# The first attention's tasks in a new order, with transposes placed between the matmuls of the projections

## The reference

```python
x = x + _L0_xattn_ref(_layernorm(x, axis=-1), ctx_1024, ctx_1024, ...)

def _L0_xattn_ref(query, key, value, w_q, b_q, w_k, b_k, w_v, b_v, w_o, b_o):
    q = query @ w_q.T + b_q
    k = key @ w_k.T + b_k
    v = value @ w_v.T + b_v
    # 16 heads of 16 features
    scores = jnp.einsum('bhqd,bhkd->bhqk', q, k) * scale
    probs = jax.nn.softmax(scores, axis=-1)
    y = jnp.einsum('bhqk,bhkd->bhqd', probs, v)
    return y @ w_o.T + b_o
```

## Time and profile before

| | |
|---|---|
| median of the timed runs | 3880.64 us |
| span of the profiled execution, first to last instruction | 3869.9 us |
| the profiled execution's own time, outside its span | not given apart; the median is 10.7 us above the span |
| TensorE busy over the span | 3678.2 us, 95% |
| VectorE, ScalarE, GpSimd busy | 3088.5, 2207.4, 2200.5 us |
| mean granted TensorE clock | 0.981 |
| 500 to 700 us (first attention): TensorE, VectorE, ScalarE, GpSimd | 196.3, 176.9, 145.6, 138.1 of 200 us |

### The profile page before, as it was taken

How to read it: one execution, slowest core, us unless ns; L and a number is a source line. 1 busy time by engine, 2 the same in 40 slices (tenths; PEclk the granted TensorE clock), 3 DMA queues, 4 the chain that set the end, 5 groups by cost and what they waited for, 6 DMA issues and landing times. The chain is left out here.

```text
span 3869.9 us, 134428 instructions
## 1 busy us (share of the span) xinstructions
PE 3678.2 (95%) x47408; PEld 2870.0 (74%) x47408; DVE 3088.5 (80%) x5266; ACT 2207.4 (57%) x4529; POOL 2200.5 (57%) x3316
## 2 busy tenths in 40 slices
PE   5999999995799999999999996999999999999999
PEld 4777777773688888888888884566666668888888
DVE  4888888885778777778777775798888977777777
ACT  3777777775444444444444442577677765555554
POOL 5666666664245443333333334466666667887777
PEclk9999999997899999999999998899999999999999
DMA  4677777774332322222222224799999952232322
GB/s 130 197 204 207 214 209 209 205 213 154 102 85 79 84 68 74 66 70 69 68 72 68 72 66 90 158 211 216 211 217 208 215 151 80 75 77 75 79 75 72
DMA packets 834241, 502.59 MB, mean 130 GB/s; under 512 B 262037, under 2 KB 824408, under 8 KB 833480
## 3 DMA queue, kind: packets, MB, share of 16 engines
q1 hardware_dynamic: 832680, 493.49, 50.5%
q0 software_dynamic: 928, 0.49, 0.1%
HBM read 251.27 MB, written 214.96 MB: 120 GB/s over the span
## 5 line engine op out<-in xcount | busy, mean ns | idle before, releaser
L1556 ACT ACTIVATE phase_spare<-phase_loop_hid,phase_b1T 128x128 f32<-128x128 f32 x2048 | 586.1, 368 | 710.9 <-PE phase_loop_hid L193 702.2
L1129 DVE TENSOR_REDUCE phase_loop_mx<-phase_loop_score 128x8 f32<-128x1024 f32 x512 | 625.4, 1222 | 98.5 <-PE phase_loop_score L882 91.0
L1522 PE MATMUL phase_loop_moe_y<-phase_w,phase_spare 128*128 x2048 | 693.6, 379 | 0.1
L1037 ACT ACTIVATE phase_loop_pt<-phase_loop_scoreT 128x1024 f32<-128x1024 f32 x448 | 458.6, 1024 | 268.3 <-PE phase_loop_scoreT L916 265.8
L1524 PE MATMUL phase_loop_moe_y<-phase_w,phase_spare 128*128 x2048 | 558.2, 273 | 0.0
L191 PE MATMUL phase_loop_hid<-phase_loop_moe_h,all_w_first_hi 128*128 128x128 f16 x2048 | 449.2, 219 | 0.0
L192 PE MATMUL phase_loop_hid<-phase_loop_moe_h,all_w_first_hi 128*128 128x128 f16 x2048 | 449.1, 219 | 0.0
L192 PE MATMUL phase_loop_hid<-phase_loop_moe_h,phase_w_hi 128*128 128x128 f16 x2048 | 449.1, 219 | 0.0
L193 PE MATMUL phase_loop_hid<-phase_loop_moe_h,all_w_first_lo 128*128 128x128 f16 x2048 | 449.1, 219 | 0.0
L193 PE MATMUL phase_loop_hid<-phase_loop_moe_h,phase_w_lo 128*128 128x128 f16 x2048 | 449.1, 219 | 0.0
L191 PE MATMUL phase_loop_hid<-phase_loop_moe_h,phase_w_hi 128*128 128x128 f16 x2048 | 449.0, 219 | 0.0
(11 more groups left out here) (293 smaller groups left out, 11038.9 us busy)
## 6 DMA issues: line engine op xcount, KB each, us to landing
qk_scratch<-phase_loop_qk SPq DMA_DIRECT2D x192, 256.0 KB, 3.4
phase_loop_cin<-in_ctx SPq DMA_DIRECT2D x128, 256.0 KB, 4.6
x_scratch<-phase_loop_x SPq DMA_DIRECT2D x128, 256.0 KB, 3.1
h_scratch<-phase_loop_hr SPq DMA_DIRECT2D x128, 256.0 KB, 3.7
phase_loop_qS<-qk_scratch SPq DMA_DIRECT2D x384, 64.0 KB, 2.8
phase_loop_kS<-qk_scratch SPq DMA_DIRECT2D x384, 64.0 KB, 2.4
ks_scratch<-ct_scratch SPq DMA_DIRECT2D x384, 64.0 KB, 2.4
all_w_first_lo<-ks_scratch SPq DMA_DIRECT2D x128, 192.0 KB, 4.0
```

The source lines that it names most:

```text
L1037: act.activation(pt[n % len(pt)][:, :, :], score_t_bank[:, :].rearrange("p (j n) -> p j n", j=HB2), ACT.Exp, scale=exp_scale).then_inc(s_e ...
L1129: v.tensor_reduce(to, score_bank[:, :].rearrange("p (h j n) -> p h j n", h=2, j=CH), AX.X, ALU.max).then_inc(s_mx.sem, 1)
L1522: pe.matmul(o[:, :], hh[n % NH][:, j, :], row, start=half == 0 and j == 0, stop=False, skip_group_check=True)
L1556: i = act.activation(hf[n % NF][:, j, :], hid(u, n)[:, j * S:(j + 1) * S], ACT.Gelu, bias=w["b1"][:, bass.ds(e * HB + (4 * half + j), 1)], ...
```

## The change

- `braid` is new: it runs one task of TensorE (the first given, a projection) as a generator, matmul by matmul, and after the matmuls whose numbers stand in `places` it puts in one matmul each of the other tasks, which are transposes of other units. `passes`, `transpose_pair`, `project`, `project_rows`, `t_max` and `y_rows` become generators for this, with the semaphore of each on its last matmul as before. The second attention gets the same instructions as before through `whole`.
- TensorE's list has the score tasks together, the av tasks together in pairs, and four braids: o with t_x and t_max, q with y1, v with t_c, k with y0 and t_y.
- `plan` and `shared` distribute the three banks anew.
- Every engine's list has a new order and new lags. On GpSimd they were bias_x 6, maxima 8, norm0 5, rstd1 12, rows1 12, in that order.
- `pt` gets three buffers in the first attention instead of two, taken in turn over units (`pt_of`).

```diff
@@ -125,7 +126,9 @@
 
     def step(tasks, s):
         for lag, task in tasks:
-            if 0 <= s - lag < count:
+            if lag is None:
+                task(s)
+            elif 0 <= s - lag < count:
                 task(Unit(0, s - lag))
     for s in range(count + depth):
         step(tasks, s)
...
@@ -191,6 +194,39 @@
     eng.matmul(out, l_hi, r_hi, start=start, stop=False)
     eng.matmul(out, l_hi, r_lo, start=False, stop=False)
     return eng.matmul(out, l_lo, r_hi, start=False, stop=stop)
+
+
+def passes(eng, out, l_hi, l_lo, r_hi, r_lo, start, stop, done=None):
+
+    yield eng.matmul(out, l_hi, r_hi, start=start, stop=False)
+    yield eng.matmul(out, l_hi, r_lo, start=False, stop=False)
+    m = eng.matmul(out, l_lo, r_hi, start=False, stop=stop)
+    if done:
+        m.then_inc(done.sem, 1)
+    yield m
+
+
+def whole(part):
+
+    def go(u):
+        for _ in part(u):
+            pass
+    return go
+
+
+def braid(count, main, places, *sides):
+
+
+    def go(s):
+        def part(lag, task):
+            return task(Unit(0, s - lag)) if 0 <= s - lag < count else iter(())
+        between = chain.from_iterable(part(*side) for side in sides)
+        for i, _ in enumerate(part(*main)):
+            for _ in range(places.count(i)):
+                next(between, None)
+        for _ in between:
+            pass
+    return None, go
 
 
 def together(nc, *programs):
...
@@ -452,13 +488,15 @@
                             self.rs[s][:, a:a + 1], ALU.subtract, ALU.mult).then_inc(self.s_xn.sem, 1)
 
 
-def transpose_pair(pe, bank, x, ident):
+def transpose_pair(pe, bank, x, ident, done):
 
     for kb in range(KB):
         for a in range(PAIR):
             at = (kb * PAIR + a) * P
             m = pe.transpose(bank[:, at:at + P], x[:, a, kb * P:(kb + 1) * P], ident)
-    return m
+            if (kb, a) == (KB - 1, PAIR - 1):
+                m.then_inc(done.sem, 1)
+            yield m
 
 
 def slot_of(buffers, u):
...
@@ -507,7 +545,10 @@
         nm = two("nm", [P, PAIR, HEADS], F32)
         m3 = two("m3", [P, PAIR, P], F16)
         mT = two("mT", [P, PAIR, S], F16)
-        pt = (two if first else four)("pt", [P, HB2, S], F32)
+        pt = [k.sb(f"pt{i}", [P, HB2, S], F32) for i in range(3 if first else 4)]
+
+        def pt_of(u, n):
+            return pt[(u.no * NP + n) % len(pt)]
         cut_by = () if first else CUT_BY_MIN + CUT_BY_PRODUCT
         yE = two("yE", [P, PAIR, 512], F32)
         rec = two("rec", [P, PAIR, HEADS], F32)
...
@@ -545,9 +586,9 @@
         s_late = k.sem("s_late")
 
         if first:
-            plan = [(3, "t_x"), (8, "t_y"), (3, "q"), (7, "y0"), (2, "t_c"), (3, "k"), (5, "t_max"), (3, "v"),
-                    (7, "y1"), (8, "o")]
-            shared = (("t_x", "y0", "y1"), ("t_y", "t_c", "t_max", "v"), ("q", "k", "o"))
+            plan = [(9, "o"), (2, "t_x"), (6, "t_max"), (3, "q"), (8, "y1"), (4, "v"), (2, "t_c"), (3, "k"), (7, "y0"),
+                    (8, "t_y")]
+            shared = (("o", "y1", "t_c", "y0"), ("t_x", "v", "t_y"), ("t_max", "q", "k"))
         else:
             plan = [(8, "t_y"), (4, "t_max"), (1, "q"), (7, "y1"), (6, "y0"), (8, "o")]
             shared = ((), ("t_max", "q", "o"), ("t_y", "y1", "y0"))
...
@@ -706,8 +747,8 @@
                         d_mp.inc(sp.dma_start(qS[u.slot4][at:at + PARTS, :, :], src), u)
 
                 if first:
-                    tasks = [(5, place_max), (3, stack_k), (2, store_q), (9, store_x1), (0, load_x), (4, store_ct),
-                             (4, store_max), (9, store_h), (0, load_c), (2, store_k), (2, stack_q)]
+                    tasks = [(4, store_k), (0, load_c), (6, store_max), (0, load_x), (9, store_x1), (4, stack_k),
+                             (6, place_max), (10, store_h), (3, store_q), (2, store_ct), (3, stack_q)]
                 else:
                     tasks = [(5, load_c), (1, load_xT), (5, store_max), (3, stack_q), (11, store_x1), (12, store_h),
                              (2, store_q), (8, load_r), (5, place_max), (2, stack_k)]
...
@@ -794,7 +835,7 @@
                     ln1.split_rows(p, u, hr[u.slot], s_hrh, s_hr)
 
                 if first:
-                    tasks = [(6, bias_x), (8, maxima), (5, norm0), (12, rstd1), (12, rows1)]
+                    tasks = [(9, rstd1), (1, norm0), (2, bias_x), (10, rows1), (5, maxima)]
                 else:
                     tasks = [(11, rows1), (4, maxima), (5, ctx_as_v), (6, cut(p, 3)), (9, rstd1)]
                 run_steps(p, tasks, units, DEPTH, **follow("gpsimd", p))
...
@@ -810,24 +851,26 @@
                 def t_x(u):
                     ln0.s_xn.wait(pe, u)
                     free("t_x", u)
-                    transpose_pair(pe, ring["t_x"], ln0.xn[u.slot], ident).then_inc(s_tx.sem, 1)
+                    yield from transpose_pair(pe, ring["t_x"], ln0.xn[u.slot], ident, s_tx)
 
                 def t_c(u):
                     d_c.wait(pe, u)
                     free("t_c", u)
-                    transpose_pair(pe, ring["t_c"], cin[u.slot], ident).then_inc(s_tc.sem, 1)
-
-                def project(u, bank, src, name, bias, ones):
+                    yield from transpose_pair(pe, ring["t_c"], cin[u.slot], ident, s_tc)
+
+                def project(u, bank, src, name, bias, ones, done):
 
                     hi, lo = w[name]
                     x = src(u)
                     for mb in range(KB):
                         o = bank[:, mb * 256:(mb + 1) * 256]
                         for kb in range(KB):
-                            three_passes(pe, o, hi[:, kb, mb * P:(mb + 1) * P], lo[:, kb, mb * P:(mb + 1) * P],
-                                         x[:, 0, kb, :], x[:, 1, kb, :], kb == 0, False)
+                            yield from passes(pe, o, hi[:, kb, mb * P:(mb + 1) * P], lo[:, kb, mb * P:(mb + 1) * P],
+                                              x[:, 0, kb, :], x[:, 1, kb, :], kb == 0, False)
                         m = pe.matmul(o, w[bias][:, mb * P:(mb + 1) * P], ones[:, :], start=False, stop=True)
-                    return m
+                        if mb == KB - 1:
+                            m.then_inc(done.sem, 1)
+                        yield m
 
                 def fold_q(u):
 
...
                 if first:
-                    tasks = [(3, make["t_x"]), (8, make["t_y"]), (7, av(2)), (5, score(3)), (7, score_t(3)),
-                             (3, make["q"]), (7, make["y0"]), (2, make["t_c"]), (7, av(3)), (6, score_t(0)),
-                             (3, make["k"]), (5, make["t_max"]), (6, av(0)), (6, score_t(1)), (4, score(0)),
-                             (3, make["v"]), (7, make["y1"]), (6, score_t(2)), (4, score(1)), (8, make["o"]),
-                             (6, av(1)), (4, score(2))]
+                    tasks = [(5, score(0)), (7, score_t(0)), (8, av(2)), (8, av(3)),
+                             braid(units, (9, make["o"]), (1, 2, 3, 4, 5, 6), (2, make["t_x"]), (6, make["t_max"])),
+                             (5, score(1)), (7, score_t(1)),
+                             braid(units, (3, make["q"]), (2, 3, 4, 5), (8, make["y1"])),
+                             (5, score(2)), (7, score_t(2)), (7, av(0)), (7, av(1)),
+                             braid(units, (4, make["v"]), (1, 2, 3, 4), (2, make["t_c"])),
+                             (5, score(3)), (7, score_t(3)),
+                             braid(units, (3, make["k"]), (1, 2, 3, 4, 8, 9, 10, 11), (7, make["y0"]), (8, make["t_y"]))]
                 else:
-                    tasks = [(6, av(0)), (3, score(0)), (8, make["t_y"]), (5, mask_score_t(0)), (4, make["t_max"]),
+                    tasks = [(6, av(0)), (3, score(0)), (8, whole(make["t_y"])), (5, mask_score_t(0)), (4, whole(make["t_max"])),
                              (5, score_t(0)), (3, mask_score(1)), (6, av(1)), (3, score(1)), (5, score_t(1)),
-                             (1, make["q"]), (7, make["y1"]), (3, mask_score(2)), (5, mask_score_t(2)), (3, score(2)),
-                             (6, av(2)), (5, score_t(2)), (6, av(3)), (3, mask_score(3)), (6, make["y0"]),
-                             (3, score(3)), (5, score_t(3)), (8, make["o"]), (2, mask_score(0))]
+                             (1, whole(make["q"])), (7, whole(make["y1"])), (3, mask_score(2)), (5, mask_score_t(2)), (3, score(2)),
+                             (6, av(2)), (5, score_t(2)), (6, av(3)), (3, mask_score(3)), (6, whole(make["y0"])),
+                             (3, score(3)), (5, score_t(3)), (8, whole(make["o"])), (2, mask_score(0))]
                 run_steps(pe, tasks, units, DEPTH, **follow("tensor", pe))
 
             @block.scalar
...
@@ -1062,9 +1110,9 @@
                         split_ahead.high(act, n)
 
                 if first:
-                    tasks = [(5, copy_y(0)), (1, hi_x), (6, hi_y), (5, expo(3)), (1, hi_q), (0, hi_c), (5, copy_y(1)),
```

(35 more changed lines are left out.)

11 lines of the change are left out of this document (7 added, 4 removed).

## The result

The changed kernel takes 4212.41 us (median, 4195.69 to 4215.62), the kernel before 3880.49 us on the same chip: ratio 1.085, 95% interval 1.083 to 1.087. The forecast was 4200 us, in a range of 4100 to 4300.

The account below looks back on a forecast made before the run. Rounds of waits through GpSimd (18.1 us) and SyncE (18.4) would bind the first attention, 19.0 us a step with the clock effect: 1064 + 52 + 17 = 1133 us against 823.6, +319 with a later start; 3880.6 + 319 = 4200 us, range 4100 to 4300.

Parts of the forecast that it names:

- round through GpSimd: First attention: t_max, VectorE, GpSimd's whole list, next t_max; no step below 18.1 us; chance of such rounds 0.80.
- round through SyncE: First attention: rows1, store_h, q and k stores and stacks, score_t(0), t_max, GpSimd; 36.9 us for two steps, 18.4 each.
- waits at t_max or scoreT: TensorE in the first attention: a wait of 4 to 6 us once a step, as a sign of being right.
- at most 1 us of GpSimd's wait for the statistics: GpSimd in the first attention: its wait for VectorE's statistics at most 1 us, as a sign of being right.
- several us of it were even named as a sign of being wrong: GpSimd in the first attention: waiting several us before rstd1 would show the forecast wrong.
- TensorE's own step: First attention: four fewer mode changes at 0.12 us, 0.5 us less, so 12.7 us if nothing else waited.
- Weaving: Transposes among TensorE's matmuls in the braids: costed at nothing; bounds 0 and 2.2 us a step.
- The 56 ns: The skill's time for a 128-column matmul; with it weaving would save 1.1 us a step, TensorE's step 11.6 us.
- The clock: Stalls in most steps bring 1.2 GHz for some 3 us of work; taken as 0.8 us a step, bounds 0 and 1.7.
- The sum: First to last addition of x: 1064 + 52 + 17 = 1133 us against 823.6; the first about 10 us later.
- The 10.7 us between span and median: Whole kernel before: span 3869.9 us against median 3880.64 us, taken as time outside the span and kept.
- The rival that was faster: First attention: TensorE stays the bound, then the chain t_y to y1, 12.9 us a step; about 3858 us; chance 0.10.

Follow-up runs that it names:

- the fourth run: Changed kernel with GpSimd's list rotated (maxima before rstd1), load_c at lag 1, store_q before store_h and store_h at lag 11: 3888.37 us, ratio 1.0032 to the kernel before.
- the new places and a second queue: Against the run with bundled transposes and stack_q in two halves: store_x1 and load_c issued by ScalarE instead of SyncE; 3862.93 us, ratio 0.9962 to the kernel before.

## Why the prediction was right

The time and the sign were right, and so was the kind of mechanism, a round of waits. But a third round, which the forecast did not have, holds TensorE and sets the place where it waits; it is nearly as long as the forecast round through GpSimd. That the number came out so close is in part luck.

- **The round through GpSimd: right in its terms.** Forecast 3.5 + 0.44 + 3.1 = 7.04 us from t_max to GpSimd's start on the second norm, measured 7.04; GpSimd's list and the way back 11.1, measured 10.64 + 0.27 = 10.91 without the 0.36 us to spare. In all 18.1 forecast against 17.95, and the shortest steps of the kernel after are 17.95. But there another round holds TensorE, and only the run with a later load_c shows this one as TensorE's wait (71.9 us in 20 steps).
- **The round through SyncE: there, but not first.** Forecast 36.9 us over two steps, 18.4 each, by way of store_h. With the two others gone a step is 17.5 us, 34.9 for two, and taking store_h out of the way ends it. In the kernel after it has time to spare: SyncE is through with k's store at 717.88 and waits until 720.12 for t_c, and stack_k stands right behind store_x1 (721.54 + 0.47 to 722.10) and waits for no landing.
- **What failed: the list of rounds.** The prediction followed store_h in SyncE's order and took load_c as an issue like others, though its lag of 0 against t_c's 2 with two buffers makes it wait for TensorE in its own step. It said that in effect of GpSimd ("a dependence can be followed by units") and did not do it for the rest of SyncE's list. That the number held is due to the near tie: had this round been 20 us instead of 18.33, 56 steps would have added some 90 us (an estimate).
- **Signs that were wrong.** It named waits at t_max or scoreT; it was score, for the stacked k. It named at most 1 us of GpSimd's wait for the statistics; it is 7.9 us a step (166.3 / 21), and several us of it were even named as a sign of being wrong. That contradicts its own round, in which all but GpSimd's 11.0 us, 7.1, must appear as that wait.
- **TensorE's own step: right.** 12.7 us was forecast, 0.12 us for each of four mode changes; with the chain widened it is 12.69 us, (13.17 - 12.69) / 4 = 0.12 us each if all of it is theirs.
- **Weaving: nothing gained, as forecast.** Transposes stand between the matmuls at the distance of 0.11 us at which everything else stands (kernel after):

```profile
704.30 0.27 PE L201 MATMUL phase_loop_ring<-phase_loop_cT,phase_wk_hi 128*128 128x256 f16 x1
704.41 0.27 PE L202 MATMUL phase_loop_ring<-phase_loop_cT,phase_wk_hi 128*128 128x256 f16 x1
704.52 0.27 PE L496 MATMUL phase_loop_ring<-all_ident,phase_loop_yn 128*128 128x128 f32 x1
704.63 0.27 PE L203 MATMUL phase_loop_ring<-phase_loop_cT,phase_wk_lo 128*128 128x256 f16 x1
...
713.80 0.22 PE L942 MATMUL phase_loop_ring<-all_ident,phase_loop_m 128*128 128x128 f16 x1
713.85 0.27 PE L201 MATMUL phase_loop_ring<-phase_wo_hi,phase_loop_yT 128*128 128x256 f16 x1
```

The Trainium skill ("TensorE: Matmul & The Clock Gate", LDWEIGHTS and Fast Weight Load) puts a weight load without the fast mode at its columns over 1.2, some 107 ns for 128 of them (an estimate by its formula); the 0.11 us agrees with that in size. The 56 ns that I took from its Back-to-back issue gap, where it is the gap of an isolated matmul, is seen behind the f16 transposes of t_max (713.80 to 713.85) and not behind the f32 ones. Whether the load or the f32 matmul itself takes the 0.11 us, no run here tells; hidden it is not.

- **The clock: present, larger than taken.** The stall and what follows it, kernel after (last three columns clock, DMA share, GB/s):

```profile
705.50:709.50 4.00, 0.17 (x2) 0.00 (x0) 1.29 (x2) 1.07 (x2) 3.95 (x4) 1.00 0.70 188
709.50:714.00 4.50, 4.42 (x61) 3.59 (x62) 2.15 (x5) 1.62 (x2) 2.84 (x8) 0.62 0.40 122
```

A mean of 0.86 with levels of 0.50 and 1.00 is 28% of the time at 1.2 GHz, 5 us a step against the some 3 assumed. What it costs can be read from score to t_max, which lies in the round through load_c: 2.67 us at clock 1.00 in the fourth run, 4.16 to 4.94 in the kernel after, so 1.5 to 2.3 us a step against the forecast 0.8. In the step shown it is 4.22, so that this round would take 18.33 - 1.55 = 16.8 us at clock 1.00 (an estimate), less than GpSimd's 17.95: the near tie is partly the clock's doing.

- **The sum.** Between first and last addition 1142.1 us (forecast 1133): 1062.1 for 56 steps (1064), 80.0 for the last seven (69). The first came 20.8 us later, not 10. In the fourth run and in the one with only load_c later it came 5.2 us later (111.7), and with only GpSimd's list changed still 22 (128.5). So 15.6 us are waits of the round through load_c while the pipeline fills, which the forecast did not have.
- **A misreading without effect.** The 10.7 us between span and median are not time outside the span: in every later run the time is 1.8 us above its span. By that the profiled execution took some 3871.7 us (an estimate), less than any of the timed ones on record then; the term dropped out of the sum.
- **The rival that was faster** (chain t_y to y1, 12.9 us) is real: it appears as TensorE's wait for add_x as soon as the rounds are gone, at 13.08 us. But near the 3858 us it promised the time came only with the new places and a second queue (3863); with the chain at 13.08 us and late stacks in other steps it was 3888.

## What to carry to other kernels

With engines that work in order, write for each pair "who waits, in which step, for which unit", and follow every such edge round, those of load tasks and buffer reuse as well: a task that waits for the very step it stands in makes everything behind it in its queue part of a round. Look for ties: of single repairs of this change one won nothing clear of noise and one made it slower (ratio 1.085 to 1.093), and three together brought it to 1.003. And when a queue shows hardly a wait but is late, look at its issues: here the two later orders of the queue brought nothing, and a second queue did.

## What I had not expected of the hardware

- The stacks' transfers cost SyncE 2.9 us for six, and SyncE's issues fill a 13 us step although the DMA share is only 0.70. What two transfers on ScalarE's queue cost that engine is not in its busy time (152.6 us of 200), which leaves issues out. The changed kernel gained 0.8% by them, while the kernel before with two became 0.16% slower, for a reason that stays open.
- The clock falls in every step between 500 and 797 us behind a stall of only 3.3 to 5.0 us, and the time at 0.50 is not always the same: some 3.4 us behind the stall that ends at 709.58, about twice as long behind others. Where the stall stands decides what the slow stretch costs: moved before t_max, it made the step longer.
- f32 transposes between f16 matmuls cost as much as side by side, 0.11 us each; woven or bundled, TensorE's quiet step is 12.69 us.
